# Four layers of a graph network: GpSimd's wait for freed rows ahead of each quad of gathers instead of ahead of four

## What is computed

```python
def layer2(x, edge_index, ...):             # attention over incoming edges, 8 heads of 16
    h = layernorm(x, ln_g, ln_b)
    xl, xr = h @ W_l + b_l, h @ W_r + b_r
    e = xl[src] + xr[dst]
    alpha = einsum(leaky(e), att)           # one score per edge and head
    a = softmax of alpha over the edges of one dst
    return x + relu(segment_sum(xl[src] * a, dst) + bias)

def layer3(x, edge_index, edge_rel_emb, ...):  # an MLP on every edge
    h = relu(concat(x[src], x[dst], edge_rel_emb) @ W1 + b1)
    agg = segment_sum(relu(h @ W2 + b2), dst)
    return layernorm(x + relu(agg @ Wn + bn), gamma, beta)

x = layernorm(x + layer1(x)); x = layernorm(x + layer2(x))
x = layernorm(x + layer3(x)); x = layernorm(x + layer4(x))
```

## Time and profile before

| | |
|---|---|
| runs, us | 5950.3, 5982.4, 5987.7; median 5982.4 |
| span of the profiled execution | 6105.3 us |
| mean granted TensorE clock | 0.688 of full |
| busy, share of the span | TensorE 52%, GpSimd 53%, VectorE 41%, ScalarE 16% |
| DMA, mean busy share of the 16 engines | 0.2 to 0.5, 84 GB/s on average |

### The profile page before, as it was taken

One profiled execution on the slowest core, in us unless ns is written; L12 is line 12 of the kernel. 1 busy time (PEld: TensorE's weight loads), 2 busy tenths in 40 slices (PEclk: granted clock), 3 DMA queues, 4 the chain that ended last, 5 costly groups with the idle time before them and its releaser, 6 DMA issues.

```text
span 6105.3 us, 52726 instructions
## 1 busy us (share of the span) xinstructions
PE 3148.5 (52%) x17147; PEld 2593.6 (42%) x17150; DVE 2498.6 (41%) x4988; ACT 968.1 (16%) x2133; POOL 3211.4 (53%) x3332
## 2 busy tenths in 40 slices
PE   3443444436656566565535565565567334433336
PEld 2333333335545455454424555455556323323324
DVE  5554555634433334333533333333334522322228
ACT  0000000122211112111111111111111301111115
POOL 6666666364544444444364544444443366666662
PEclk8555555677777777777757777777778655666557
DMA  3141111134444444444233333333333211111112
GB/s 87 45 134 44 46 46 46 45 94 123 127 117 122 114 124 120 117 122 111 71 95 97 98 100 97 93 101 93 100 98 84 69 47 46 44 46 45 46 45 70
DMA packets 601180, 514.20 MB, mean 84 GB/s; under 512 B 99694, under 2 KB 532781, under 8 KB 600910
## 3 DMA queue, kind: packets, MB, share of 16 engines
q0 software_dynamic: 105248, 216.15, 13.9%
q10 hardware_dynamic: 210704, 154.61, 9.6%
q1 hardware_dynamic: 284958, 140.08, 8.4%
HBM read 410.93 MB, written 91.26 MB: 82 GB/s over the span
## 4 chain that ended last, share of the span: by engine, by line
another core or an unknown queue 37%; PE 24%; DVE 16%; issue 13%; ACT 5%; ACTq 2%; DVEq 1%; POOL 1%; DMA 1%; SPq 0%; POOLq 0%
PE bank L690 22%; DVE acc L1504 4%; DVE work L1542 3%; PE bank L695 2%; DVE bank L1527 2%; DVE quads L1517 1%; ACT acc L1092 1%; DVE quads L1529 1%; DVEq L375 1%; ACTq L1126 1%; ACT quads L1251 1%; ACTq L1121 1%; ACT quads L1219 1%; ACTq L1129 0%
## 5 line engine op out<-in xcount | busy, mean ns | idle before, releaser
L690 PE MATMUL bank<-quads,work 128*128 128x128 f32 x3920 | 656.2, 313 | 919.5 <-issue 589.3
L690 PEld LDWEIGHTS bank<-quads,work 128*128 128x128 f32 x3920 | 599.3, 223 | 1078.1 <-issue 731.7
L1504 DVE TENSOR_TENSOR acc<-bank,acc 128x512 f32 x588 | 403.2, 686 | 1323.2 <-remote 1063.4
L1100 ACT COPY bank<-zeros 128x384 f32<-128x384 f32 x588 | 283.4, 483 | 2104.6 <-DVE acc L1504 1423.0
L582 POOL DMA_INDIRECT g<-xl,srct x392 | 377.2, 962 | 450.4 <-DVE msg L1828 332.4
L582 POOL DMA_INDIRECT g<-a_src,srct x392 | 377.6, 963 | 442.6 <-PE bank L690 324.6
L582 POOL DMA_INDIRECT nodes<-xl,srct x390 | 374.1, 959 | 380.5 <-DVE msg L1828 265.3
L582 POOL DMA_INDIRECT nodes<-a_src,srct x390 | 374.1, 959 | 358.1 <-PE bank L690 232.7
L1913 DVE TENSOR_TENSOR msg<-bank,b_b 128x512 f32<-128x512 f32 x196 | 135.6, 692 | 994.9 <-PE bank L690 557.5
L582 POOL DMA_INDIRECT g<-x,srct x392 | 371.2, 947 | 240.7 <-issue 116.4
L690 PE MATMUL bank<-quads,g 128*128 128x128 f32 x1568 | 351.9, 393 | 282.7 <-issue 182.1
(11 more groups left out here) (377 smaller groups left out, 6082.1 us busy)
## 6 DMA issues: line engine op xcount, KB each, us to landing
partial<-acc ACTq DMA_DIRECT2D x196, 288.0 KB
work<-local_rank ACTq DMA_DIRECT2D x392, 128.0 KB
work<-xr_by_rank SPq DMA_DIRECT2D x784, 64.0 KB
work<-b_by_rank SPq DMA_DIRECT2D x784, 64.0 KB
work<-in_rel_t ACTq DMA_DIRECT2D x196, 128.0 KB
g<-acc SPq DMA_DIRECT2D x126, 64.0 KB, 1.9
g<-in_x,srct POOLq DMA_INDIRECT x392
scan_penalties<-work SPq DMA_DIRECT2D x14, 448.0 KB
```

The costliest lines, as they stand in the source:

```text
L690: return nc.tensor.matmul(to, lhsT, rhs, start=start, stop=stop, skip_group_check=True)
L1100: nc.scalar.copy(partial_bank(l, i)[:, P:QE].rearrange("p (t e) -> p t e", e=P), zeros[:, 0:P].unsqueeze(1).broadcast_to([P, TQ - 1, P])). ...
L1504: v.tensor_tensor(window, partial_bank(l, q)[:, :], window, ALU.add).then_inc(partial_copied, 1)
```

## The change

`GATHER_QUADS` becomes a table by layer: 4 in the first and the fourth layer as before, 1 in the second and the third. There GpSimd waits ahead of each quad from the fifteenth on, for the one slot that this quad needs. The gathers, their order and all other engines' programs stay. The count asked for is capped at the number of quads, which changes none of the values that occur.

```diff
-GATHER_QUADS = 4
+GATHER_QUADS = {0: 4, 1: 1, 2: 1, 3: 4}
...
-        assert NQ % GATHER_QUADS == NQ % PE_QUADS == NQ % DVE_QUADS == NQ % SP_QUADS == 0
+        assert NQ % PE_QUADS == NQ % DVE_QUADS == NQ % SP_QUADS == 0
...
+                ahead = GATHER_QUADS[l]
...
                 for i in range(NQ):
-                    if i % GATHER_QUADS == 0 and i + GATHER_QUADS > RING:
-                        pool.wait_ge(rows_used, before + i + GATHER_QUADS - RING)
+                    if i % ahead == 0 and i + ahead > RING:
+                        pool.wait_ge(rows_used, before + min(i + ahead, NQ) - RING)
                         pool.sem_inc(pool_step, 1)
                     for t in range(tiles_of(i)):
                         pool.indirect_dma_start(
```

## The result

The changed kernel takes **5486.7 us** (median of four runs, 5483.8 to 5491.5) where the kernel before takes 5977.1 (four runs, 5950.3 to 5987.7; three of them are those of the table above): a ratio of 0.919, interval 0.916 to 0.922. The forecast was 5715 us and its range began at 5500. So the sign and the mechanism came out as argued, the gain is 490 us where 267 were worked out, and the time lies outside the range. And it is no gain everywhere: on another chip, as the experiments show, the kernel before already takes 4493 us and the change gives nothing.

What follows compares the result with a forecast made beforehand. TensorE's finished work is seen late while GpSimd's gathers run on. Shorter runs save 0.56 (second layer) plus 0.94 us (third), 1.50 x 182 = 273 us, 267 after scaling: 5982 - 267 = 5715 us; range 5500 to 6040.

Steps and rivals of the forecast that it cites:

- What bounds the kernel: Second and third layer: TensorE's finished work is seen late while gathers run on; 8.26 and 8.14 us a quad.
- The runs: Gathers on end would fall from four quads to two or one: 13.6 or 8.6 us third layer, 14.6 or 9.6 second.
- the clearing time: Second and third layer: held reports of TensorE come out 3.1 us after a run's last gather.
- The restart: GpSimd, second and third layer: a wait that holds costs 0.74 us before gathers start again.
- nine pairs in ten: Nine quads of ten in two-quad runs, the rest single: 7.0 us a quad third layer, 7.5 second.
- the rival of single quads: Every run a single quad: 8.6 us third layer, 9.6 second; 328 us more, 6300 us; chance 12%.
- The factor 0.980: Whole kernel: median of the runs over the profiled span; scales the saving from 273 to 267 us.
- The cost of meeting VectorE: Second and third layer: gathers slowed beside VectorE's L1551, 0 to 0.4 us a quad, 0.2 taken.
- The clock: TensorE's granted clock in the second and third layer: 0.8 of full or a little less, from 0.74 and 0.75.
- No change: Rival, 12%: TensorE is held as long as gathers run, however cut up; 8.1 us a quad, 5950 to 6010 us.
- slower: Rival, 12%: every run a single quad, each paying 3.1 us of clearing and 0.74 of restart; 6300 us.
- Much faster: Rival, 8%: reports hardly held without long runs, GpSimd the bound at 5.76 us a quad; 870 us saved, 5110.

Runs made afterwards that it cites:

- e12: Kernel before, with second-layer waits per quad for a count three quads later, third-layer 3.02 us pauses between a group's quads, fourth-layer waits per quad: 5662.7 us against 6158.1.
- e13: Kernel before, with one gather of four in the second layer and plain SP-queue transfers of other rows in the third: 4640.9 us on the held chip.
- e8: The kernel before, unedited, profiled again on a chip where TensorE's reports are not held: 4491.8 us.

## Why the prediction was right in sign and short in size

**What bounds the kernel: right for its chip.** That reports of TensorE are held for as long as gathers run was read from the earlier trace rows, without an experiment. e12 (pauses that make the stage shorter) and e13 (no gather, no late report) show it. That it is TensorE's reports and nobody else's shows in the trace of before: 380 waits end on "remote" there (171 of ScalarE, 152 of VectorE, 57 of GpSimd), and all of them wait for a semaphore that TensorE raises. It was stated of "the kernel", though, and on three of the four chips of the experiments it does not hold. Nothing in the trace of before could have told this, and it doesn't touch the forecast, which was for the conditions of the recorded runs. What the reports meet on a held chip, and whether the product or its report is late, no run here tells.

**The runs: right, with other shares and prices.** The starts of the changed kernel's gathers from the fifteenth quad on, grouped by the length of the run that they begin (a run ends where GpSimd pauses for over 0.6 us ahead of a quad), give:

| layer, run | predicted | measured, mean start to start | runs |
|---|---|---|---|
| third, two quads | 13.6 us | 12.35 | 51 |
| third, one quad | 8.6 | 6.45 | 77 |
| second, two quads | 14.6 | 12.41 | 39 |
| second, one quad | 9.6 | 6.93 | 27 |
| second, three quads | not foreseen | 21.57 | 25 |

*The step that failed is the clearing time.* The prediction put 3.1 us behind each run, read from a run of 16 gathers, and used it for runs of 4 and 8 as well. In the changed kernel's third layer all 51 runs of two quads do end on a late report, but it comes 1.6 us behind the last gather (median; 0.6 to 2.0). Of the 77 runs of one quad only 24 end on one, at 1.0 us (median); behind the other 53 nothing is late, GpSimd waits for TensorE's work itself. In the kernel before, 42 of 44 groups ended on one, at 2.9 us (median). The shorter the run, the shorter the clearing, and behind one quad there is mostly none. The restart was right: 0.75 us (0.74 assumed). With it the gap from the last gather's end to the next run's start is 1.7 us after one quad and 2.3 after two, where 3.1 + 0.74 = 3.8 were assumed. In the second layer, where 4.9 us were assumed with the 1.04 us of exponential and weighing, it is 2.1 and 2.4.

By the table, pairs cost 6.2 us a quad and singles 6.45 in the third layer, so that the question on which much of the working hung, nine pairs in ten or fewer, hardly mattered. It was also answered wrong: 102 of the 179 quads counted were in pairs. In the second layer 75 quads of 180 were in runs of three, at 7.2 us a quad. By the same prices the rival of single quads would have given not 8.6 us but 6.45 in the third layer.

*The sum by the measured prices.* (8.25 - 6.75) + (8.13 - 6.27) = 3.36 us a quad, not 1.50; times 182 it is 612 us of the 620 us by which the profiled executions differ (6105.3 and 5484.9).

*The factor 0.980 was a wrong step too, in the other direction.* The profiled execution of before was 128 us above the median of its runs; that of after is 2 below its own. The difference of the medians is 490 us, of the profiled executions 620. I had scaled the saving by 2%. But outside the two stages the executions differ by 8 us only, so the excess of 128 us most likely lay within them, in what the saving was read from; no second profile of before in these conditions shows it. The two errors had opposite signs: with the right prices my sum would have been 612 x 0.980 = 600 us, 5382, now 105 us too low. The range's upper end had a slip of its own: seven in ten in pairs and 0.4 us make the second layer 0.13 us a quad slower (8.4 against 8.26), which was put at nothing, some 23 us.

**The cost of meeting VectorE: refuted.** 0.2 us a quad were added for gathers beside L1551. A gather's mean in the changed kernel is 962 to 965 ns in the third layer and 971 to 973 in the second, against 959 to 963 and 959 to 962 before (963 in the earlier trace rows): next to nothing, and some 0.05 us a quad. Nor did nearly every quad come to meet it: in the third layer 58 gathers took over 1.1 us before and 63 after, all of them beside that instruction; in the second, with few exceptions beside it too, 33 and 85. By the shared port pair of the Trainium skill (SBUF — State Buffer) a gather could have waited for a whole instruction of VectorE. This trace doesn't bear out the prices that the prediction took from it: of the third layer's 782 gathers none takes more than 1.19 us, 0.25 above the usual 0.94, where L1552 lasts 0.47.

**The clock.** "0.8 or a little less" came true in the second layer (0.80) and was too low in the third (0.86). With one gather a quad and with none it is 0.98 and 0.99 (e13), in e8 on a free chip 0.96 and 0.97: it was higher in the stages in which TensorE stood still for less.

**The rivals.** No change, slower: neither occurred, and e12's third layer excludes the first one's reason, that only the share of gathers in the time counts; there GpSimd gathers 5 of 7.3 us, where it was 5 of 8.1, and held reports cost the period nothing. Much faster, 5110 us: not reached, but the part that the forecast missed lies on its side. It named the right limit with the wrong number: with no report held GpSimd's bound is 5.08 us a quad (e8), not 5.76, which late reports had already made longer.

**What would show it.** Gathers in runs of 4 or 8: yes in the third layer, and 12 as well in the second. Starts every 13.6 and 14.6 us: 12.3 and 12.4. ScalarE's longest steady idle time ahead of the expansion 5 to 6 us: up to 7.7 (7.05 above), so longer; 18.7 before. Both stages shorter, the third more; first and fourth as before: yes.

## What to carry to other kernels

Where waits end on "remote" shortly after another engine's burst of indirect gathers, cut the burst or put other work into it: a run of 16 gathers in place of 4 or 8 cost 1.5 to 1.9 us of 8 a quad here. A finer wait only cuts a run if it holds; where it is satisfied, as in the fourth layer, it does nothing. Try such a change on more than one chip: this one is worth 8% where it was recorded and nothing on the free chip that it ran on.

## What the hardware showed that was not expected

The same program takes 4491 to 4496 us on three chips, 6158 on a fourth, and 5977 where the recorded runs were made. Gathers and VectorE's instructions last the same on both kinds (967 and 963 ns for a gather, 688 and 686 for L1504). What differs is when TensorE's finished work is seen. On a free chip 782 gathers on end delay nothing; on a held chip the second layer is 8.25 us a quad in place of 5.08, the fourth 5.76 in place of 5.03. With no gathers a held chip has the pace of a free one (4.53 and 4.56 us a quad).

The held traces show one thing more: there, records of semaphore updates are missing wherever GpSimd gathers, those of VectorE too, although no wait for it ends on "remote". Of VectorE's 4024 updates the trace of before has 2746 and that of e8, on a free chip, 4020. In the third layer's edge stage before has 627 of 917, and e13, the held chip without gathers, 976 of 976. How this is tied to the late reports stays open.

What sets a chip apart was not found. The held chip was met once, with two kernels, so it isn't shown either that it is the chip and not a state that passes.
